# Making the product dt·u of blocks 2 to 15 on GpSimd in place of VectorE

## The reference, cut to what matters

```python
xz = x @ Wi.T + bi
x_in, z = (xz[..., :D_INNER], xz[..., D_INNER:])          # D_INNER = 512
xc = conv_general_dilated(x_in, conv_w, causal, 4 taps, per channel) + conv_b
u = silu(xc)
dt = softplus(x_in[..., :DT_RANK] @ Wdt.T + bdt)
A = -exp(A_log)                                           # 512 channels x 16 states
def step(h, inp):
    dt_t, u_t = inp
    h = h * exp(dt_t[:, :, None] * A[None]) + dt_t[:, :, None] * Bm[None] * u_t[:, :, None]
    y = einsum('bdn,dn->bd', h, Cm)
    return (h, y)
out = scan(step) * silu(z)
x = x + out @ Wo.T + bo + layernorm(x) * Dv.mean()
```

## Time and profile before

| | |
|---|---|
| median of 3 runs | 746.35 us |
| the profiled execution's own time | 746.69 us |
| its span, first to last instruction | 744.9 us |
| PE / DVE / ACT / POOL busy | 641.2 / 644.0 / 616.2 / 328.1 us |
| recurrence on VectorE (L1246) | 535.9 us of full-width groups, 38.5 us of half ones that start from a saved state |
| TensorE's granted clock | 0.922 of full speed, mean |

### The profile page before, as it was taken

One profiled execution on the slowest core, in us unless ns is written; L12 is line 12 of the kernel. 1 busy time (PEld: TensorE's weight loads), 2 busy tenths in 40 slices (PEclk: granted clock), 3 DMA queues, 4 the chain that ended last, 5 costly groups with the idle time before them and its releaser, 6 DMA issues.

```text
span 744.9 us, 8294 instructions
## 1 busy us (share of the span) xinstructions
PE 641.2 (86%) x2928; PEld 332.6 (45%) x2928; DVE 644.0 (86%) x431; ACT 616.2 (83%) x1089; POOL 328.1 (44%) x184
## 2 busy tenths in 40 slices
PE   7867897799886999997988999995986999699857
PEld 5632442264342365644424466441231664156435
DVE  2427846979999999999979999899999999999961
ACT  2487998779988998999778989999898879884763
POOL 0107202436797066888900737436991060160010
PEclk9997998999997899999888999998896999799979
DMA  8440737171739051252559060251526241614001
GB/s 294 157 169 15 241 135 233 64 230 50 289 98 321 7 212 44 108 175 86 204 138 329 28 234 0 95 189 58 197 88 195 97 158 58 225 54 173 29 1 56
DMA packets 40026, 103.08 MB, mean 138 GB/s; under 512 B 4080, under 2 KB 13040, under 8 KB 39984
## 3 DMA queue, kind: packets, MB, share of 16 engines
q1 hardware_dynamic: 37424, 94.40, 35.3%
q10 hardware_dynamic: 2560, 8.14, 5.0%
HBM read 23.08 MB, written 4.19 MB: 37 GB/s over the span
## 4 chain that ended last, share of the span: by engine, by line
PE 43%; ACT 29%; DVE 14%; DMA 7%; issue 5%; POOL 1%; ACTq 1%; SPq 0%; POOLq 0%; DVEq 0%
ACT G L1133 12%; DVE G L1246 12%; PE Y L1424 9%; PE MB L1448 6%; PE MB L1391 5%; PE MB L1287 4%; PE MB L1369 4%; PE MB L1350 3%; ACT XN L950 3%; DMA XI<-XI 3%; ACT XI L1050 2%; PE MB L1402 2%; PE MB L1444 2%; DMA RV<-DW 2%; PE MB L1359 2%
## 5 line engine op out<-in xcount | busy, mean ns | idle before, releaser
L1246 DVE TENSOR_TENSOR_SCAN G<-G,RV 128x1024 f32<-128x1024 f32 (+3 forms) x256 | 535.9, 2156 | 33.3 <-ACT G L1133 20.6
L1133 ACT ACTIVATE G<-RD,COL 128x1024 f32<-128x1024 f32 (+1 forms) x288 | 279.4, 1043 | 17.7 <-PE Y L1424 15.3
L1424 PE MATMUL Y<-G,RW 128*32 128x512 f32 x1024 | 139.7, 661 | 39.3 <-DVE G L1246 39.3
L855 POOL TENSOR_SCALAR LV<-LV 128x4 f32<-128x4 f32 x18 | 18.3, 1015 | 232.3 <-ACT XN L950 232.1
L864 POOL TENSOR_TENSOR LV<-LV,HALF 128x4 f32<-128x4 f32 (+1 forms) x25 | 47.3, 1891 | 118.2 <-DVE LV L1196 116.7
L895 POOL TENSOR_SCALAR X<-X,LV 128x256 f32<-128x256 f32 x32 | 88.3, 2770 | 0.8
L1391 PE MATMUL MB<-XI,DIAG 128*64 128x512 f32 x248 | 69.7, 704 | 13.0 <-DMA XI<-XI 13.0
L1424 PEld LDWEIGHTS Y<-G,RW 128*32 128x32 f32 x1024 | 27.3, 116 | 116.3 <-issue 58.2
L881 POOL TENSOR_SCALAR XN<-X,LV 128x256 f32<-128x256 f32 x36 | 76.7, 2136 | 1.9
L1350 PE MATMUL MB<-MT,XF 128*128 128x256 f32 x240 | 58.3, 386 | 7.6 <-ACT XF L976 3.9
L1448 PE MATMUL MB<-WO,ZS 128*128 128x256 f32 x256 | 64.0, 383 | 0.0
(11 more groups left out here) (94 smaller groups left out, 785.7 us busy)
## 6 DMA issues: line engine op xcount, KB each, us to landing
RD<-DW SPq DMA_DIRECT2D x60, 512.0 KB, 3.8
RV<-DW SPq DMA_DIRECT2D x60, 512.0 KB, 5.1
W<-in_w SPq DMA_DIRECT2D x48, 256.5 KB, 3.8
XI<-XI ACTq DMA_DIRECT2D x30, 256.5 KB, 5.7
X<-in_x SPq DMA_DIRECT2D x8, 512.0 KB, 6.2
out<-X SPq DMA_DIRECT2D x7, 512.0 KB, 3.0
G<-in_w SPq DMA_DIRECT2D x4, 513.0 KB, 7.7
RV<-in_w SPq DMA_DIRECT2D x4, 513.0 KB, 12.3
```

The lines of the kernel that those rows point to most:

```text
L1133: eng.activation(G[:, i % NG, 1 + t0:1 + t1], RD[:, q, t0:t1], ACT.Exp, scale=NAC[:, states(i):states(i) + 1]).then_inc(sems["exp"])
L1246: eng.tensor_tensor_scan(g[:, at:1 + t1], g[:, at:1 + t1], v[:, at:1 + t1], first, ALU.mult, ALU.add).then_inc(sems["scan"])
L1424: ins = eng.matmul(Y[32 * q:32 * q + 32, 512 * h:512 * h + 512], RW[:, states(i + o), :], G[:, (i + o) % NG, 512 * h + 1:512 * h + 513], s ...
```

## The change: what it does

The product of blocks 2 to 15 is issued by GpSimd and no longer by VectorE; blocks 0 and 1 (three instructions: two halves and a whole) stay on VectorE. It is the same operation with the same operands, waits and semaphore, at the same place in the list. Fourteen instructions of 128 x 1024 move.

```diff
@@ -894,6 +894,14 @@
                         eng.wait_ge(sems["skips"], (count.value["skip", a] + 3) // 4)
                     eng.tensor_scalar(v[:, i, :], v[:, i, :], lv[:, 5, i:i + 1], lv[:, 6, i:i + 1],
                                       ALU.mult, ALU.add).then_inc(sems["skip"])
+                elif stage == "w" and a[0] > 1:
+                    k, p = a
+                    t0, t1 = span(k, p)
+                    for hf in halves(k, p):
+                        e.wait_ge("u", k, hf)
+                    e.wait_ge("dt", k, p)
+                    d = DW[:, 1, t0:t1]
+                    eng.tensor_tensor(d, d, DW[:, 0, t0:t1], ALU.mult).then_inc(sems["w"])
                 elif stage == "msv":
                     g, = a
                     e.wait_ge("mv", g)
@@ -1218,7 +1226,7 @@
                         ins = eng.tensor_scalar(xn[:, i, :], v[:, i, :], lv[:, 3, i:i + 1], lv[:, 4, i:i + 1],
                                                 ALU.mult, ALU.add)
                     ins.then_inc(sems["vnorm"])
-                elif stage == "w":
+                elif stage == "w" and a[0] < 2:
                     k, p = a
                     t0, t1 = span(k, p)
                     for hf in halves(k, p):
```

## The result

The changed kernel takes 783.02 us (779.8 to 784.85, three runs) against 746.35: ratio 1.0495, interval 1.0465 to 1.0525, 36.7 us slower. I had forecast 754 and a range to 767. The profiled execution has a span of 783.1 us, 38.2 more.

A forecast was written before the change was run, and what follows sets the result against it. VectorE's queue was taken to bound the stretch from 160 to 725 us. Terms -12.5 - 3.0 + 17.6 + 5.4 = +7.5 us on 746.69 gave 754.2, forecast as 754 us; range 742 to 767, the forecast's own 749.5 to 759.

The forecast's parts named there:

- I take 1.6: Recurrence beside each GpSimd product: VectorE loses 1.6 us, at 11 blocks 17.6 us more (bounds 1.7 and 27.5).
- Rival 1: Recurrences beside products: GpSimd's whole instruction holds VectorE, about 764 us (761 at 2.2 us each), range 759 to 771; chance 0.25.
- the late part: Blocks 4 and 12: products behind GpSimd's own work delay the first exponentials, 1.6 + 3.8 = 5.4 us more (4 to 10).
- the net of this part: VectorE at 11 blocks: 17.6 us more from holds against 12.5 us less from products taken off it.
- At most blocks GpSimd is free soon after the old time: GpSimd's queue: products late only at blocks 4 and 12; elsewhere `repd` wait for the previous block's last exponentials.
- `msv` at nothing: Behind block 4's product: `msv` 4.6 us late moves the reduction about 1.5 us, within VectorE's stand of 1.6; nothing added.
- The sign that was to tell of it: TensorE's transposes behind block 4: a wait longer than 5 us would say `msv` was undercounted.
- The 3 us from block 8's wait: VectorE ahead of block 8's product: 3 of the 3.81 us wait for `u` gained, between 0 and 3.8.
- rival 4: GpSimd's product starved between recurrences: 34 us each, 25 us late at 14 blocks, over 1000 us; chance 0.06.

The follow-up runs named there:

- the run without inputs: Kernel before, products on VectorE, plus 14 GpSimd fills of 1000 bfloat16 elements that read nothing, at the products' places: 746.43 us, ratio 1.0024.
- the kernel with ten products: Changed kernel with the products of blocks 4, 8, 10 and 12 back on VectorE, the other ten on GpSimd: 752.62 us, ratio 1.0119.
- The run with dt first: Changed kernel with SyncE's order altered: a block's four copies of dt to RD stand ahead of its product's first copy: 761.81 us, ratio 1.0240.
- the run with the products moved ahead: Changed kernel with the products of blocks 4, 7, 8, 10 and 12 further ahead in GpSimd's own order: 761.14 us, ratio 1.0224.

## Why the prediction was wrong

- **The bound and the sign were right.** VectorE paces the middle, a product on GpSimd holds it, and the change is slower.
- **The hold was mis-sized.** "I take 1.6" scaled the growth of a recurrence beside an operation of 256 elements by eight. It is 2.1 to 2.2 us, and it fell on 12 recurrences, not 11. The trace had the better guide in the length of the operation itself: 2.39 us alone holds 2.18, 1.05 us holds 0.83. The rule that I set aside (the Trainium skill, "SBUF — State Buffer", section "SBUF: two separate sides", the pair is held for the whole instruction) is met by these to some 0.2 us. Its other half, that only a GpSimd operation that reads excludes a VectorE operation with two SBUF inputs, is met exactly by the run without inputs. Rival 1 had the hold nearly right (2.5 or 2.2 us), yet its 764 us is 19 short, because the late part was wrong in it too. The forecast had the net of this part at 17.6 - 12.5 = 5.1; VectorE's busy time grew by 9.9, and the kernel with ten products, which has no late one, costs 8.9.
- **"At most blocks GpSimd is free soon after the old time" failed at blocks 8 and 10.** For block 10 the prediction matched no times on the two engines. Two rows of the trace before give it away, a product on VectorE at 467.14 and the norm ahead of it in the list on GpSimd at 475.94. Engines that walk one list are at different places of it at one time, and VectorE was ahead of GpSimd. That step is 11.2 us, and moving the one product ahead gave 10.5 back. At block 8 GpSimd's second run of skips started 12 us later than the 9.9 us of delay explain (383.08 for 361.31), and the correction and the product behind it with them; the step is 3.6 us, 1.5 of it idle time.
- **The late part at blocks 4 and 12 left out a path: 5.6 + 8.4 us for 1.6 + 3.8.** Only the wait of a block's first recurrence for its first exponential was priced. At block 12 that term was right, 3.74 us for 3.8; at block 4 it was nothing. The prediction then took the rest of the block to be in time. For the exponentials that nearly holds: the second is done at 245.49 us where VectorE is free at 247.42, and at block 12 at 601.54 for 600.68. But the second copy of the product, which the prediction does not have, stands behind the four of dt, and it ended the waits of 4.17 and 3.54 us. The four of dt took 8.4 us at block 4 to land, not 3.8. The run with dt first shows what this order costs: with block 4's product as late, the step fell from 5.6 to 1.3 us, and at block 12 from 8.4 to 2.4.
- **`msv` at nothing.** The sign that was to tell of it came: TensorE waits 6.48 us at the transposes behind block 4, over the 5 us named.

```profile
243.24 1.09 PE L1305 MATMUL MB<-COL,MS 128*128 128x128 f32 x4 [6.48 <-POOL MS L909]
```

  At block 4 VectorE did not wait for it but for the copy. In the run with the products moved ahead it was, at block 8.
- **The 3 us from block 8's wait weren't there.** Taking that wait away by itself gave nothing; the copy of the product took its place, the end at 0 of my bound.
- The sum by what was measured: 9.9 us busier and 28.3 us more of idle time make the 38.2 of the span; 27.2 of the idle time and 1.6 of the busy time lie in the four stretches.

## What to carry to other kernels

An operation moved to another engine at the same place of a list takes over what stands ahead of it there, waits included; find the place by matching times on both engines, not by counting rows. On the path its price is more than its own lateness: whatever stands in the waiter's queue behind it is late as well, here the copies of dt and then the product's own second copy. Moving it ahead has a price too, the lateness of what it overtakes. Where VectorE runs recurrences with two inputs from SBUF, count a GpSimd operation that reads as time of VectorE, nearly its whole length.

## What the hardware showed that I had not expected

- The hold of a recurrence follows the inputs: none for a fill, 0.8 us for 1000 elements of one input, 2.1 us for 1000 or 1024 of two, that is 0.8 ns an element read with one and 1.05 with two. A fill did hold VectorE's one-input normalising, by 0.87 us.
- A product on GpSimd is quick when it comes first, 2.36 to 2.42 us against 1.2 us on VectorE; it is 4.3 us when it must let a recurrence end. It was never starved (rival 4): a long operation waits once and then keeps VectorE out.
- VectorE can absorb a part of such holds: 26.5 us more of recurrences cost 18.3 us, as its waits for exponentials shrank.
